# A graph network kernel: the edge sort in one unrolled stage, with the normalisation and the QKV projection beside its scatter

## The reference, cut to what matters

```
x = x + _L0_gnn_ref(_layernorm(x, axis=-1), edge_index, edge_type_64, ...)

def _L0_gnn_ref(node_features, edge_index, edge_relations, query_emb, Wq, bq, Wk, bk, Wv, bv, rel_w, ...):
    enh = node_features + 0.1 * query_emb[None, :]
    Q = (enh @ Wq + bq).reshape(N, H, D)
    K = (enh @ Wk + bk).reshape(N, H, D)
    V = (enh @ Wv + bv).reshape(N, H, D)
    src, dst = (edge_index[0], edge_index[1])
    rel = rel_w[edge_relations]
    mod_k = K[src] + 0.2 * rel[:, None, :]
    scores = jnp.einsum('ehd,ehd->eh', Q[dst], mod_k) / D ** 0.5
    seg_max = jax.ops.segment_max(scores, dst, num_segments=N)
    ...
    agg = jax.ops.segment_sum(w[:, :, None] * V[src], dst, num_segments=N)
```

## Time and profile before

| What | Value |
|---|---|
| median of 3 runs | 4443.25 us (4440.49 to 4446.23) |
| profiled execution, its own time | 4487.6 us |
| span of the profiled execution | 4485.3 us |
| mean granted clock of TensorE | 0.851 |
| busy share of the span: PE, PEld | 64%, 44% |
| busy share: DVE, ACT, POOL | 58%, 26%, 33% |
| stage "scatter" (172 to 771 us), POOL busy | 476.23 us of 599 |
| stages between the reload and `build_links` (810 to 1015 us) | 205 us |

### The profile page before, as it was taken

One profiled execution on the slowest core, in us unless ns is written; L12 is line 12 of the kernel. 1 busy time (PEld: TensorE's weight loads), 2 busy tenths in 40 slices (PEclk: granted clock), 3 DMA queues, 4 the chain that ended last, 5 costly groups with the idle time before them and its releaser, 6 DMA issues. The chain is left out here.

```text
span 4485.3 us, 51375 instructions
## 1 busy us (share of the span) xinstructions
PE 2850.3 (64%) x12855; PEld 1975.5 (44%) x12856; DVE 2600.5 (58%) x5649; ACT 1158.0 (26%) x4271; POOL 1490.9 (33%) x1406
## 2 busy tenths in 40 slices
PE   4555553164677777531069358888888539899970
PEld 4344443153445545221057235555555337677750
DVE  7766664245888888436721359888989820022221
ACT  0000000000555555401012024444444212233320
POOL 0377776004555555000000034444444105011114
PEclk9999999985887788565589679999999759999995
DMA  0000002515665666010000033333333126211112
GB/s 29 2 4 4 4 4 9 74 57 166 177 183 172 176 176 175 29 66 2 14 20 0 25 110 108 104 103 105 106 102 107 42 70 102 47 33 34 33 36 75
DMA packets 236031, 323.43 MB, mean 72 GB/s; under 512 B 114940, under 2 KB 166560, under 8 KB 235609
## 3 DMA queue, kind: packets, MB, share of 16 engines
q0 software_dynamic: 83488, 220.74, 18.9%
q1 hardware_dynamic: 117971, 95.44, 8.0%
q10 hardware_dynamic: 34402, 5.30, 1.0%
HBM read 287.87 MB, written 32.86 MB: 72 GB/s over the span
## 5 line engine op out<-in xcount | busy, mean ns | idle before, releaser
L1253 POOL DMA_INDIRECT g_rows<-h_d,src x416 | 397.1, 954 | 1328.0 <-SPq L1200 812.8
L925 POOL DMA_INDIRECT a_strip<-kv_d,src x416 | 430.4, 1035 | 593.8 <-POOLq L74 262.4
L484 POOL DMA_INDIRECT rec_d<-rec_s,place x400 | 476.2, 1191 | 243.6 <-issue 216.8
L949 ACT ACTIVATE x<-a_strip,x 128x64 f32<-128x64 f32 x1664 | 408.5, 334 | 221.6 <-PE a_psv L994 197.6
L994 PE MATMUL a_psv<-x 128*125 128x260 f32 x832 | 306.2, 502 | 158.0 <-DVE agg L1088 121.0
L384 PE MATMUL ps_base<-start,lo_hot_t 125*125 125x25 f32 x800 | 184.7, 384 | 264.1 <-DVE picked L439 263.4
L384 PEld LDWEIGHTS ps_base<-start,lo_hot_t 125*125 125x125 f32 x800 | 175.4, 326 | 341.2 <-issue 339.7
L1330 PE MATMUL g_psa<-g_msg,g_hot 128*125 128x256 f32 x832 | 249.7, 426 | 109.3 <-DVE g_msg L1422 109.3
L1318 PE MATMUL g_pso<-w_o,g_ut 128*128 128x256 f32 x832 | 284.3, 424 | 1.9 <-ACT g_lk L1268 1.9
L1590 PE MATMUL ps_h_f<-h_t,w_f 128*128 x640 | 174.5, 434 | 161.7 <-DMA b_f<-in_L_ffn_b 136.8
L994 PEld LDWEIGHTS a_psv<-x 128*125 128x125 f32 x832 | 178.2, 238 | 221.9 <-DVE agg L1088 118.1
(11 more groups left out here) (373 smaller groups left out, 5661.7 us busy)
## 6 DMA issues: line engine op xcount, KB each, us to landing
a_row<-rows_d SPq DMA_DIRECT2D x104, 256.0 KB
e_w<-in_L_ffn_W1p SPq DMA_DIRECT2D x8, 1024.0 KB
e_w<-in_L_ffn_W2p SPq DMA_DIRECT2D x8, 1024.0 KB
y_d<-e_y SPq DMA_DIRECT2D x56, 128.0 KB, 1.7
a_strip<-kv_d,src POOLq DMA_INDIRECT x416
g_rows<-h_d,src POOLq DMA_INDIRECT x416
rec_d<-rec_s,place POOLq DMA_INDIRECT x400
x<-in_x SPq DMA_DIRECT2D x2, 3125.0 KB
```

Of the source, the lines that this page charges most:

```text
L484: pool.indirect_dma_start(out=m.rec_d[:, :], out_offset=bass.IndirectOffsetOnAxis(ap=place[b][:, u:u + 1], axis=0), in_=rec_s[b][:, u, :], ...
L925: pool.indirect_dma_start(out=strip[:, lane.start + u, place:place + 2, :].rearrange("p a d -> p (a d)"), out_offset=None, in_=m.kv_d[:, : ...
L949: act.activation(msg[b][:, u, h, 0:HD], strip[:, lane.start + u, place, h * HD:(h + 1) * HD], ACT.Copy, scale=w[:, k * U + u, h:h + 1])
L1253: pool.indirect_dma_start(out=rows[r][:, u, 64:512], out_offset=None, in_=m.h_d[:, :], in_offset=bass.IndirectOffsetOnAxis(ap=m.src[:, s * ...
```

## The change

`build_sort` becomes one block without hardware loops, and the normalisation and the projection become part of it.

- **Layout.** An edge's partition is now its number divided by 400 and its column the rest (`per_row`), so edges are loaded as 125 partitions of 400, and the fields need no turning. `hi` comes from a multiplication by 1/125 with corrections: nine chained instructions on 125 x 400. PE turns only `dst` and `lo`, and SP stores them to `dst_rows_d` (f32) and `lo_rows_d` (bf16).
- **Histogram.** The operands of PE are swapped (`hi_hot` is the weight, `lo_hot` the 125 columns that move), and the result is transposed once. `hi_hot` is made in four parts between the steps.
- **Scatter.** In each step SP loads the 500 destinations and the 500 `lo` to all 125 partitions by two broadcast DMAs (`row`, `row_lo`, three buffers each); PE's spreading is gone. The four rank instructions each cover 125 columns. PE counts with widths of 100, 75, 50 and 25 columns, so that `run` holds the running counts after each of the four columns; `look` reads them. POOL's four indirect DMAs read `rec_in` itself, ACT's copy is gone, and `place` has four buffers.
- **Beside the scatter** (`beside` on DVE, `slot` on the others): moments of two node tiles a step in steps 0 to 12, normalisation of two tiles a step in steps 14 to 26, the store of the normalised rows at SP's step 30, and from step 20 one node tile in three steps through transposes, ACT's copy, products of V and K together (512 columns) and Q (256), bias, split and store. The query embedding is multiplied with the weights once and joins the biases. The numbering of the 416 tiles runs on 104 partitions in step 1.
- The stages "x", `layer_norm` "n0", "qkv", `scale_qkv` and `project` "qkv" go. `build_reload` and `build_links` are unchanged.

```diff
--- before.py
+++ after.py
-def build_sort(nc, m, a):
+def build_sort(nc, m, a, x_room, rows, vec, half):
+    NE_T = E // P
+    ST = NE_T // U
+    NB = 4
+    BT = NE_T // NB
+    RR, RP, RK = 3, 4, 3
+    STATS, NORM, QKV = 0, 14, 20
...
+        @block.sync
+        def _(sp):
...
+            sp.wait_ge(s_turned, 2)
+            sp.dma_start(m.dst_rows_d.rearrange("(b i) e -> i b e", b=NB), turned[:, :, :]).then_inc(s_stored, 16)
+            sp.dma_start(m.lo_rows_d.rearrange("(b i) e -> i b e", b=NB), turned_b[:, :, :]).then_inc(s_stored, 16)
+            sp.dma_start(m.x[:, :, :], rows(a["x"])).then_inc(s_x, 16)
+            sp.dma_start(w_vk[:, :, 0:D], half(a["L0_gnn_Wv"])).then_inc(s_w, 16)
...
+            sp.wait_ge(s_stored, 32)
+            for s in range(ST):
+                r = s % RR
+                if s >= RR:
+                    sp.wait_ge(s_rank, s - RR + 1)
+                sp.dma_start(row[r][:, :], m.dst_rows_d[U * s:U * s + U, :].rearrange("(o u) e -> o (u e)", o=1)
+                             .to_broadcast([P, U * P])).then_inc(s_row[r], 16)
+                sp.dma_start(row_lo[r][:, :], m.lo_rows_d[U * s:U * s + U, :].rearrange("(o u) e -> o (u e)", o=1)
+                             .to_broadcast([P, U * P])).then_inc(s_row[r], 16)
...
+                if s == NORM + 16:
+                    sp.wait_ge(s_norm, NT)
+                    sp.dma_start(rows(m.n_d), m.h[:, :, :]).then_inc(s_out, 16)
+                j = slot(s, QKV + 4)
+                if j is not None:
+                    sp.wait_ge(s_take, 2 * j + 1)
+                    sp.dma_start(m.kv_d[j * P:(j + 1) * P, :], kv[j % RK][:, :]).then_inc(s_kvout[j % RK], 16)
...
+            for s in range(ST):
+                pool.wait_ge(s_place, s + 1)
+                pool.sem_inc(s_go, 1)
+                for u in range(U):
+                    pool.indirect_dma_start(
+                        out=m.rec_d[:, :], out_offset=bass.IndirectOffsetOnAxis(ap=place[s % RP][:, u:u + 1], axis=0),
+                        in_=rec_in[:, U * s + u, :], in_offset=None).then_inc(s_sent[s % RP], 16)
...
+            def histogram(s):
+                pe.wait_ge(s_hot, s + 1)
+                if s % (ST // NB) == 0:
+                    pe.wait_ge(s_hi, s // (ST // NB) + 1)
+                for u in range(U):
+                    t = U * s + u
+                    last = pe.matmul(ps_q[0:NT, 0:P], hi_hot[:, t, :], lo_hot[s % 2][:, u, :], start=t == 0,
+                                     stop=t == NE_T - 1, skip_group_check=True)
+                last.then_inc(s_used, 1)
+
+            def count(s):
+                pe.wait_ge(s_hot, ST + s + 1)
+                if s:
+                    pe.wait_ge(s_run, s)
+                for u in range(U):
+                    last = pe.matmul(ps_cnt[0:P, u * NT:U * NT].rearrange("p (v n) -> p v n", n=NT),
+                                     lo_hot[s % 2][:, u, :],
+                                     hi_hot[:, U * s + u, None, :].to_broadcast([P, U - u, NT]),
+                                     start=u == 0, stop=u == U - 1, skip_group_check=True)
+                last.then_inc(s_cnt, 1)
+
+            def look(s):
+                b = s % 2
+                pe.wait_ge(s_run, s + 1)
+                if s >= 2:
+                    pe.wait_ge(s_pick, 2 * s - 2)
+                for u in range(U):
+                    table = run[b][:, u - 1, :] if u else run[1 - b][:, U - 1, :] if s else start[:, :]
+                    last = pe.matmul(ps_base[b][0:P, u * NT:(u + 1) * NT], lo_hot_t[b][:, u, :], table,
+                                     start=True, stop=True)
+                last.then_inc(s_look, 1)
...
+            for s in range(-1, ST):
+                if s + 1 < ST:
+                    count(s + 1)
+                    look(s + 1)
...
+                j = slot(s, QKV)
+                if j is not None:
+                    pe.wait_ge(s_norm, j + 1)
+                    if j:
+                        pe.wait_ge(s_ht, j)
+                    for k in range(2):
+                        last = pe.transpose(ps_t[:, k * 128:k * 128 + P], m.h[:, j, k * 128:(k + 1) * 128],
+                                            m.ident[0:P, 0:P])
+                    last.then_inc(s_tr, 1)
+                j = slot(s, QKV + 1)
+                if j is not None:
+                    pe.wait_ge(s_ht, j + 1)
+                    if j:
+                        pe.wait_ge(s_take, 2 * j)
+                    else:
+                        pe.wait_ge(s_bias, 2)
+                    for k in range(2):
+                        pe.matmul(ps_vk[0:P, :], h_t[j % 2][:, k, :], w_vk[:, k, :], start=k == 0, stop=k == 1)
+                    for k in range(2):
+                        last = pe.matmul(ps_q[0:P, 0:D], h_t[j % 2][:, k, :], w_q[:, k, :], start=k == 0, stop=k == 1)
+                    last.then_inc(s_mm, 1)
...
+            for s in range(ST):
+                if s % (ST // NB) == 0:
+                    ts = slice(U * s, U * s + BT)
+                    dve.tensor_tensor(hi_hot[:, ts, :], m.iota[0:P, None, 0:NT].to_broadcast([P, BT, NT]),
+                                      hi[:, ts, None].to_broadcast([P, BT, NT]), ALU.is_equal).then_inc(s_hi, 1)
+                if s >= 2:
+                    dve.wait_ge(s_used, s - 1)
+                hot(s, s % 2)
...
+            def prepare(s):
+                b, r = s % 2, s % RR
+                hot(s, b)
+                dve.wait_ge(s_row[r], 32 * (s // RR) + 32)
+                dve.tensor_scalar(lo_hot_t[b].rearrange("p u q -> p (u q)"), row_lo[r][:, :], m.part[0:P, 0:1], None,
+                                  ALU.is_equal)
+                if s:
+                    dve.wait_ge(s_rank, s)
+                if s >= 2:
+                    dve.wait_ge(s_place, s - 1)
+                for u in range(U):
+                    last = dve.scalar_tensor_tensor(junk[:, u, :], row[r][:, u * P:(u + 1) * P],
+                                                    dst_f[:, U * s + u:U * s + u + 1], m.before[0:P, 0:P],
+                                                    ALU.is_equal, ALU.mult, accum_out=earlier[b][:, u:u + 1])
+                last.then_inc(s_rank, 1)
+
+            def add_counts(s):
+                b = s % 2
+                dve.wait_ge(s_cnt, s + 1)
+                if s:
+                    dve.wait_ge(s_run, s)
+                    dve.wait_ge(s_look, s)
+                before = run[1 - b][:, U - 1, :] if s else start[:, :]
+                dve.tensor_tensor(run[b][:, :, :], ps_cnt[0:P, 0:U * NT].rearrange("p (u n) -> p u n", n=NT),
+                                  before[:, None, :].to_broadcast([P, U, NT]), ALU.add).then_inc(s_run, 1)
+
+            def settle(s):
+                b = s % 2
+                dve.wait_ge(s_look, s + 1)
+                dve.tensor_tensor(picked[:, :, :], ps_base[b][0:P, 0:U * NT].rearrange("p (u n) -> p u n", u=U),
+                                  hi_hot[:, U * s:U * s + U, :], ALU.mult).then_inc(s_pick, 1)
+                dve.wait_ge(s_pick, 2 * s + 1)
+                dve.tensor_reduce(base[:, :], picked[:, :, :], AX.X, ALU.add).then_inc(s_pick, 1)
+                if s >= RP:
+                    dve.wait_ge(s_sent[s % RP], 16 * U * (s // RP))
+                dve.wait_ge(s_rank, s + 1)
+                dve.wait_ge(s_pick, 2 * s + 2)
+                dve.tensor_tensor(place[s % RP][:, :], base[:, :], earlier[b][:, :], ALU.add).then_inc(s_place, 1)
...
+            def beside(s):
...
+                if s < NORM - 1:
+                    for j in (2 * s, 2 * s + 1):
+                        if j < NT:
+                            dve.bn_stats(stats[:, j, :], m.x[:, j, :]).then_inc(s_stat, 1)
...
+                if NORM <= s < NORM + 13:
+                    for j in (2 * (s - NORM), 2 * (s - NORM) + 1):
+                        if j < NT:
+                            normalise(j)
...
+                j = slot(s, QKV + 2)
+                if j is not None:
+                    dve.wait_ge(s_mm, j + 1)
...
+                    dve.tensor_tensor(kv[j % RK][:, :], ps_vk[0:P, :], b_vk[:, :], ALU.add).then_inc(s_take, 1)
...
+                    dve.tensor_tensor(qf[j % 2][:, :], ps_q[0:P, 0:D], b_q[:, :], ALU.add).then_inc(s_take, 1)
+                for k in range(2):
+                    j = slot(s, QKV + 3 + k)
+                    if j is not None:
+                        dve.wait_ge(s_term, 3 * j + k + 1)
+                        dve.tensor_tensor(qf[j % 2][:, :], qf[j % 2][:, :], m.q[:, j, k, :], ALU.subtract
+                                          ).then_inc(s_left, 1)
+
+            dve.wait_ge(s_pre, START)
+            prepare(0)
+            add_counts(0)
+            for s in range(ST):
+                if s + 1 < ST:
+                    prepare(s + 1)
+                    add_counts(s + 1)
+                settle(s)
+                beside(s)
...
```

(7 more changed lines are left out.)

653 lines of the change are left out of this document (287 added, 366 removed).

## The result

| | before | after |
|---|---|---|
| median, same chip | 4444.74 us, 4 runs (4440.49 to 4450.39) | 4224.59 us, 4 runs (4221.38 to 4227.08) |
| ratio after to before | | 0.9504, 95% interval 0.9487 to 0.952 |
| profiled execution, its span | 4487.6, 4485.3 us | 4227.08, 4225.4 us |
| mean granted clock of PE | 0.851 | 0.793 |

The kernel is 220 us faster; 4200 was forecast, with 4155 to 4285 as the range. In the two profiled executions `build_links` starts 223.6 us earlier (1015.35, now 791.71).

The account below looks back on a forecast made before the run. POOL's indirect DMAs bound the scatter, with no engine half busy from 810 to 1015 us. Terms -57 + 16 - 204.5 = -245.5 gave 4242 us profiled, 4200 by the runs; forecast 4160 to 4240, range 4155 to 4285.

Parts of the forecast that it names:

- signs that it set for being right: First indirect DMA near 115 us, 400 in 600 to 620, DVE waiting at `place` for landed DMAs, `build_links` near 770.
- term 5: Reload to `build_links`: the stages between vanish, `build_links` follows the cast after 1.3 us; gain 204.5 us.
- Step 1: Prelude up to the first scatter: first indirect DMA at 115.4 instead of 172.76 us, gain 57; wrong after 125 or before 100.
- the handshake with PE stays: Histogram: DVE and PE still hand over four products a step, so 80 us taken, with 66 and 84 as ends.
- Step 2: Scatter: POOL's 400 indirect DMAs stay at 597.8 us, other engines fit under 5.98 a step; wrong if POOL waits for `place`.
- The step outgrows POOL's 5.98 us while the projection runs: Rival, scatter beside projection: 75 steps longer by 0.6 us, 45 us in all, giving 4245; chance 0.11.
- Four `place` buffers for two ... nothing: Scatter: four `place` buffers lengthen a queue that POOL never found empty, so they gain nothing.
- Step 3: Row loads in the scatter: 4.8 of 5.98 us on five DMA engines, hidden; normalised rows' store costs 0, at most 10.
- Step 4: Scatter: indirect DMAs starting inside DVE's two-SBUF-input instructions wait for their rest; 16 us for 400, 0 and 75 kept.
- the locked phase: Rival, scatter: starts lock onto DVE's two-input instructions at their worst, 75 us for 16, giving 4258; chance 0.13.
- Two inputs in SBUF: Scatter: DVE instructions with two SBUF inputs delay POOL's DMAs; only `lo_hot` before, now the four ranks too.
- Step 5: Reload to `build_links`: reload and cast stay, gain 204.5 us; wrong if any projection work stands behind the last scatter.

Follow-up runs that it names:

- kv_late: Changed kernel with SP's store of K and V two steps later in its list; ratio 0.9451 to the kernel before, on the slower chip.
- no_q_product: Changed kernel with PE's products for Q left out, so part of the computation is missing; ratio 0.9477 to the kernel before.
- four_rows: Changed kernel with four buffers for the edge rows in place of three; ratio 0.9513 to the kernel before.
- two_places: Changed kernel with two `place` buffers in place of four; ratio 0.9547 to the kernel before.
- both: Changed kernel with the K/V store two steps later and the normalised rows stored in 25 pieces behind the K/V stores; ratio 0.9436 to the kernel before.
- sort_first: Changed kernel with the node work behind the scatter instead of beside it, in the same block; ratio 0.9722 to the kernel before.
- nd_act: Changed kernel with the store of the normalised rows issued from ACT's queue instead of SP's; ratio 0.947 to the kernel before.
- after_again: Changed kernel once more without an edit, for a common chip; ratio 0.9506 to the kernel before.
- kv_late_hot: Changed kernel with the K/V store two steps later and the scatter's `lo_hot` made by four tensor_scalar of 125 columns; ratio 0.9402 to the kernel before.

## Why the prediction was right, and where not

The sum came out at -223.6 up to `build_links` against -245.5, by these terms:

| Term | forecast, us | measured | off by |
|---|---|---|---|
| 1, first indirect DMA at | 115.4 | 103.65 | -11.7 |
| 2 and 3, the 400 DMAs, steps and loads | 597.8 | 596.5 + 38.1 idle | +36.8 |
| 4, late starts | 16 | 11.0 | -5 |
| 5, last DMA to `build_links` | 40.3 | 42.4 | +2.1 |

Together +22. Off by 22 us, times 0.990, from 4200 gives 4222; 4224.59 was measured.

That lies in the forecast's own range, 4160 to 4240, but not by its mechanism alone. Two of the signs that it set for being right failed: the 400 DMAs took 645.6 us and not 600 to 620, and `build_links` came at 791.7 and not near 770. The 11.7 us that the prelude gave back are luck; without them and the 5 us of late starts the same sum gives some 4238, at the range's very end. What was right is the large part: the work behind the scatter vanished (term 5) and the prelude shrank, and POOL's own 597.8 us stayed.

*Step 1* was mis-sized in one term, and the first DMA at 103.65 is inside the bounds of the test. Loads, chain and `hi_hot` take 16.24 + 3 x 2.75, 24.5, and 8 + 5 + 10.6 were forecast. The histogram took 76.8 us less the 8.3 of `hi_hot` inside it, 68.5, not 80. I argued that the handshake with PE stays. It stays and costs nothing: PE's weights are now the 25 columns of `hi_hot` instead of 125 of `lo_hot`, its weight loads are busy for 33.07 us instead of 58.41, and DVE goes from one `lo_hot` to the next at its own 0.68 us. That the operands are the reason is read from the diff; before, the histogram was also a hardware loop of two steps, and no run separates the two. I priced the handshake from the row and asked about neither.

*Step 2* failed. "The step outgrows POOL's 5.98 us while the projection runs", the rival given 0.11 and 45 us, is what happened: 38.1 us of idle, with 27 of them in the cycle and 11 at n_d, the normalised rows' store. Its test ("POOL waits for `place`") showed it. Each engine's busy time fits in 5.98, as I summed: DVE was busy for 52% of the time from 190 to 750 us, PE too. What I did not sum is the chain that goes through four engines and a queue: the wait for K/V stands ahead of the next row load (L287 ahead of L271), and the products ahead of the count. I took the products at 2.7 us on the ground that the clock was 1.00 before. It was 0.60, and they took 5.7. The round was 19.4 us; 3 us less would have left it under 17.9. Opening either side was enough (`kv_late`, `no_q_product`), a buffer was not (`four_rows`). That the low clock alone closes the ring is worked out from this and not shown, since no run had the ring at full clock.

"Four `place` buffers for two ... nothing" is wrong as well: `two_places` lost 11 us of scatter. It was right while POOL was never starved, and it isn't so now.

*Step 3.* The test (DVE waits for `row`) showed it wrong for a reason it did not price. The loads do hide: in `kv_late` there is one wait, in `both` none, at the same bytes. Their price held as well: in `sort_first`, where only row loads were added to the scatter, the DMA share rose from 0.09 to 0.27, and 0.18 of sixteen engines are 2.9; 17.6 engine-us in 5.98 us, the forecast, are 2.9. They were late because of where they stood. The n_d store cost 10.6 against "0, at most 10". Its cover was judged in microseconds of buffers, but in SP's queue nothing went past it (`nd_act`), and the K/V store behind it was held too.

*Step 4* held in size: 11.0 us here and 12.8 in `after_again`, 17.5 in `two_places` and 19.8 in `sort_first`; 16 was taken, and the locked phase never appeared. The rule of the delay (the rest of DVE's instruction less 0.13) fits here, 0.48 less 0.13 against 0.35 late:

```profile
182.44 0.67 DVE L459 TENSOR_TENSOR o_lo_hot<-iota,o_lo 125x500 bf16<-125x500 f32 x1
182.63 1.54 POOL L307 DMA_INDIRECT rec_d<-o_rec_in,o_place  x1 [0.30 <-issue]
```

It has limits that the prediction did not see. Its own first example misses it: the first DMA of the scatter began with 0.24 us of `lo_hot` left and was late by 0.29, and the first of the changed kernel is off in the same way (0.20 left, 0.25 late). And not every start inside such an instruction was late: in the changed kernel and `kv_late`, 45 of 54 starts in the first 0.08 us of `lo_hot` or `lo_hot_t` were not, with up to 0.71 us left. Before, 39 starts fell into `lo_hot`, 37 of them with at most 0.11 left and none of those late: that is the locked phase at zero of which the prediction speaks.

"Two inputs in SBUF" was too narrow: in `kv_late_hot` the 15 starts inside `lo_hot_t` (one input, read from PSUM before and from SBUF now) were late by 0.18 us in the mean, and making `lo_hot` with one input cured little of the whole.

The Trainium skill, page "SBUF — State Buffer", section "Who interferes with whom", adds to the two-input rule that `tensor_scalar` can enter modes that take the shared ports, and that `tensor_reduce` never does; the trace agrees with both (0.18 us above, and 0.00 in the 28 starts of `kv_late` inside L521). The prediction used only half of that rule.

*Step 5* held: 1.3 us from cast to `build_links`, and nothing of the projection behind the scatter. The last K/V store was no wait.

## What to carry to other kernels

Work laid beside a bound engine is hidden only if, besides each engine's busy time, the longest ring of waits fits in the period: follow one item through every engine and queue until it meets itself, and take the durations at the low clock too. In a queue that several streams share, a wait for fresh data belongs behind the loads that others need, and a large store in another queue. More buffers help only where the wait is for a buffer.

## What the runs showed of the hardware

- The granted clock stood at 1.00 through the scatter before (PE busy 54% of the time) and in `sort_first` (40%). In every kernel with the node work beside it, it stood at 0.50 to 0.71 in stretches of 50 us from 200 to 650 us (PE busy 52% in the changed one). In the changed kernel it fell at 182 us, in an idle time of PE of 5.4 us, at the first step after the products for the biases. Idle times as long stand in `sort_first` at 1.00 (5.5 and 6.4 us), and `two_places` fell as well, so neither the idle time nor the ring explains it, and by the first line the busy share does not either. It stays open.
- POOL's indirect DMA was late when it began inside a DVE instruction reading only SBUF: over the 400 of `kv_late` by 0.19 us in the mean of 42 starts inside `lo_hot`, 0.07 of 25 inside `lo_hot_t`, 0.02 of 73 inside the ranks. In that trace and the changed kernel's, 74 starts well inside `lo_hot` or `lo_hot_t` were late by the instruction's rest less 0.13 us, to within 0.02 us; 8 with 0.13 us or less left were not late, nor were 45 of the 54 in the first 0.08 us. In `kv_late` it was not late in 46 starts inside instructions with an operand from PSUM (L512, L518, L591, L594), nor in 28 inside a reduction over SBUF (L521).
- Two chips differ by 1.1% on the same kernel (4444.7 and 4492.5 us). The difference lies behind `build_links` (3466 to 3480 us on the slower, 3416 to 3445 on the faster ones), while the first indirect DMA came at 103.6 to 103.9 us on all. The ratio of the changed kernel was 0.9504 and 0.9506 on two of the faster chips; it was not measured on the slower one.
- The issue of a DMA on SP takes longer behind others in its queue: 0.25 us for 24 of the 25 K/V stores of the changed kernel, up to 3.3 us for the loads of a third row pair in a row, 17.9 us behind a store of 3.2 MB, and 0.25 us with that store in ACT's queue.
